# Attention on TensorE: value products issued ahead of later scores, and the turn of the value sums in four single transposes

## The reference, cut to what matters

```python
# x: (2, 1024, 128), 16 heads of 8, two batches: 32 heads
q = x @ Wq
latent_kv = (x @ Wk + x @ Wv) @ W_down_kv
k_rec, v_rec = latent_kv @ W_up_k, latent_kv @ W_up_v
scores = einsum('bhqd,bhkd->bhqk', qh, kh) * scale
decay = exp(-0.01 * 0.01 * abs(idx[:, None] - idx[None, :]))
attn = softmax(clip(scores) * decay)
out = einsum('bhqk,bhkd->bhqd', attn, vh) @ Wo
```

## Time and profile before

| what | value |
|---|---|
| median of 3 runs | 1020.47 us |
| lowest, highest | 1020.0, 1024.17 us |
| profiled execution, its time | 1019.52 us |
| profiled execution, its span | 1017.8 us |
| granted clock of TensorE, mean | 0.989 |
| TensorE busy | 947.4 us (93%) |
| ScalarE busy | 791.9 us (78%) |
| VectorE busy | 765.0 us (75%) |
| GpSimd busy | 235.8 us (23%) |

### The profile page before, as it was taken

How to read it: one execution, slowest core, us unless ns; L and a number is a source line. 1 busy time by engine, 2 the same in 40 slices (tenths; PEclk the granted TensorE clock), 3 DMA queues, 4 the chain that set the end, 5 groups by cost and what they waited for, 6 DMA issues and landing times.

```text
span 1017.8 us, 19514 instructions
## 1 busy us (share of the span) xinstructions
PE 947.4 (93%) x5246; PEld 641.9 (63%) x5246; DVE 765.0 (75%) x1700; ACT 791.9 (78%) x1368; POOL 235.8 (23%) x375
## 2 busy tenths in 40 slices
PE   5498888889889999999999999999998998999997
PEld 2221222222255888888888888888885997888885
DVE  6533333333368899999999999999997887699997
ACT  6599999999968777887787787778785775755554
POOL 3767975554670000000000000000005113100000
PEclk9799999999999999999999999999999999999999
DMA  5659979787722877777767776777631000043421
GB/s 137 183 174 281 284 251 265 233 259 246 250 85 73 305 234 239 251 231 242 253 226 243 252 234 236 253 232 243 244 107 62 1 1 2 19 134 109 129 88 42
DMA packets 96457, 186.50 MB, mean 183 GB/s; under 512 B 10636, under 2 KB 55308, under 8 KB 96396
## 3 DMA queue, kind: packets, MB, share of 16 engines
q1 hardware_dynamic: 96212, 185.33, 56.9%
q10 hardware_dynamic: 192, 0.52, 0.2%
HBM read 149.84 MB, written 35.98 MB: 183 GB/s over the span
## 4 chain that ended last, share of the span: by engine, by line
PE 74%; ACT 15%; DVE 5%; issue 2%; POOL 2%; DMA 1%; ACTq 0%; SPq 0%; DVEq 0%; POOLq 0%
PE bank L1553 30%; PE bank L1566 17%; ACT ring L1033 11%; PE bank L1560 8%; PE bank L1419 8%; PE bank L1441 4%; PE bank L1450 1%; DVE stats L1806 1%; PE bank L1680 1%; PE bank L1690 1%; DMA k_stack<-k_parts 1%; DVE state L2160 1%; POOL rstd L736 1%; DVE bank L1955 1%; POOL m_norm L907 0%
## 5 line engine op out<-in xcount | busy, mean ns | idle before, releaser
L1553 PE MATMUL bank<-xh,w_parts 128*128 128x512 f32 x896 | 276.7, 390 | 1.3 <-ACT xn L1190 1.3
L1123 ACT ACTIVATE bank<-bank 128x512 f32<-128x512 f32 x320 | 186.3, 582 | 90.1 <-PE bank L1553 90.0
L1033 ACT ACTIVATE ring<-bank 128x1024 f32<-128x1024 f32 x256 | 239.5, 1021 | 12.2 <-DVE bank L1955 11.7
L2064 DVE TENSOR_TENSOR bank<-bank,ring 128x512 f32<-128x512 f32 x320 | 223.9, 700 | 26.2 <-ACT bank L1123 3.9
L1566 PE MATMUL bank<-hh,w_parts 128*128 128x512 f32 x768 | 237.1, 390 | 0.0
L2053 DVE TENSOR_TENSOR hl<-bank,hh 128x512 fp32r<-128x512 f32 x320 | 217.9, 681 | 0.1
L1553 PEld LDWEIGHTS bank<-xh,w_parts 128*128 128x128 f32 x896 | 167.2, 188 | 38.5 <-POOL xl L914 1.7
L1117 ACT ACTIVATE hh<-bank 128x512 fp32r<-128x512 f32 x320 | 190.1, 594 | 0.5 <-DVE bank L2064 0.5
L1955 DVE TENSOR_TENSOR bank<-bank,corner 128x128 f32<-128x128 f32 x256 | 63.9, 295 | 167.2 <-PE bank L1419 167.0
L1553 PE MATMUL bank<-xl,w_parts 128*128 128x512 f32 x448 | 174.4, 389 | 0.0
L1566 PEld LDWEIGHTS bank<-hh,w_parts 128*128 128x128 f32 x768 | 144.0, 188 | 30.7 <-ACT hh L1117 1.0
(11 more groups left out here) (320 smaller groups left out, 1023.6 us busy)
## 6 DMA issues: line engine op xcount, KB each, us to landing
ring<-c_rows SPq DMA_DIRECT2D x172, 512.0 KB, 4.8
w_parts<-w_pairs SPq DMA_DIRECT2D x160, 128.0 KB, 2.9
w_pairs<-xh SPq DMA_DIRECT2D x16, 768.0 KB, 5.4
w_pairs<-xl SPq DMA_DIRECT2D x16, 512.0 KB, 3.9
big<-in_w_exp SPq DMA_DIRECT2D x16, 384.0 KB, 5.9
q_stack<-q_parts SPq DMA_DIRECT2D x32, 192.0 KB
w_ffn_parts<-xl SPq DMA_DIRECT2D x16, 384.0 KB, 4.9
w_parts<-w_ffn_parts SPq DMA_DIRECT2D x16, 384.0 KB, 3.1
```

The costliest lines, as they stand in the source:

```text
L1033: act.activation(ring[:, c % RING * S:(c % RING + 1) * S], wide[(m + c) % SB][:], ACT.Exp, bias=-BOUND).then_inc(exp_done, 1)
L1123: act.activation(bank(4 + c % ZB), bank(4 + c % ZB), ACT.Silu).then_inc(silu_ready, 1)
L1553: ins = pe.matmul(out_, w[i], x_[j], start=start and k == 0, stop=stop and k == 2, skip_group_check=not start)
L2064: dve.tensor_tensor(bank(4 + c % ZB), bank(4 + c % ZB), cb[u][:, g * GW:(g + 1) * GW], ALU.mult).then_inc(hid_ready, 1)
```

## The change

In `body`, the products of step p are issued ahead of the scores of step p + 2. `turn` now issues one transpose; it is called at the end of steps 1 to 4, where it follows the scores of that step. The wait for the evacuated sums stands ahead of the first of the four, the signal behind the last, as before. In the last turn after the loop the four are issued one after the other. No other engine's program changes.

```diff
-                def turn(i, s, half_):
+                def turn(i, s, t):
 
-                    if half_ == 0:
+                    if t == 0:
                         ready(pe, evac_ready, i)
-                    for t in range(2 * half_, 2 * half_ + 2):
-                        ins = pe.transpose(bank(7 - s)[:, t * P:(t + 1) * P], evac[1 - s][:, t * P:(t + 1) * P], ident[:])
-                    if half_ == 1:
+                    ins = pe.transpose(bank(7 - s)[:, t * P:(t + 1) * P], evac[1 - s][:, t * P:(t + 1) * P], ident[:])
+                    if t == 3:
                         ins.then_inc(evacT_psum, 1)
 
                 def body(j, b, last=False):
                     for p in range(QT):
+                        products(j, b, p)
                         if not last or p + 2 < QT:
                             two_scores(j, b, p + 2)
-                        products(j, b, p)
-                        if p in (2, 4):
-                            turn(j * 6 + b, b % 2, p // 2 - 1)
+                        if 1 <= p <= 4:
+                            turn(j * 6 + b, b % 2, p - 1)
...
-                for half_ in range(2):
-                    turn(NH // 2, 0, half_)
+                for t in range(4):
+                    turn(NH // 2, 0, t)
```

## The result

The changed kernel takes 1024.2 us (median of 20 runs, 1022.26 to 1028.13), the kernel before 1020.51 us beside it. The ratio is 1.0033, interval 1.0024 to 1.0042: 3.4 us slower, between 2.4 and 4.3 (the two medians themselves are 3.7 us apart). The forecast was 1.0 us slower, 1021.5 in all, with 1019.5 to 1023.5 as its own range. The sign was right and so was the loop that was to cause it, the size was not: 1024.2 lies above that own range, and within the whole one only because that reached to 1025.0, most of the way to rival B.

The account below looks back on a forecast made before the run. ScalarE's exponentials were taken to bound attention. Fifteen passes at 15.00 instead of 14.97 us (0.5) plus 0.5 in the first pass, added to the median 1020.5, gave 1021.5; own range 1019.5 to 1023.5, whole range 1017.6 to 1025.0.

Parts of the forecast that it names:

- rival B: Attention: a wait of 0.07 us exposed in every step, passes of 15.28, 1025.7 us in all; chance 0.08.
- What bounds the stage: Attention: ScalarE's exponentials, 0.92 us apart, set the pace; TensorE's lateness costs 0.25 us of a 14.97 us pass.
- two losses of 0.06: Attention before the change: twice a pass, a pair of transposes delays the next exponential by 0.06 us; the change removes both.
- The loop through the products: Attention: odd exponential, products, scores, even exponential three places on would take 2.80 us against ScalarE's 2.76.
- I take 0.97: Attention, TensorE: time from products' start to scores' start, put at 0.97 us between 0.87 and 0.99.
- taken as 0.04: First products of a pass: two extra waits, for loaded values and finished head, cost 0 to 0.08 us, taken as 0.04.
- its own upper case: Attention: products to scores at 0.99 and both extra waits paid give passes of 15.12, 2.3 us slower.
- The first pass: First attention pass, TensorE at half clock: scores behind products come 0.6 us late; 0.5 us lost.
- The turn behind the scores: Attention steps 1 to 4: a single transpose with handover, some 0.21 us, is covered with 0.14 us of waiting.
- The weight loads pulled ahead: Attention, TensorE: weights loaded ahead of matmuls in flight would make the handover free, products to scores 0.87 us.
- rival A: Attention: the handover is hidden, products to scores takes 0.87, passes 14.74, 1017.6 us in all; chance 0.14.
- Rival C: First attention pass: TensorE's clock rises later, two more half-clock steps, 1023.5 us in all; chance 0.08.

Follow-up runs that it names:

- turn_only: Kernel before with only the turn split into four single transposes at the end of steps 1 to 4, scores still ahead of products; 1017.76 us, ratio 0.9973.
- half_columns: waits_first with each value product taking 256 instead of 512 queries in seven of a pass's eight steps (output not the reference's); 1019.96 us, ratio 0.9986.
- waits_first: Changed kernel with a pass's first products waiting for loaded values and finished head ahead of the exponential, not behind it; 1021.9 us, ratio 1.001.
- written_out: Changed kernel with all sixteen of TensorE's attention passes written out instead of partly run in a hardware loop; 1022.69 us, ratio 1.0011.
- order_only: Kernel before with only the products moved ahead of the scores, the turn still two pairs of transposes after steps 2 and 4; 1023.56 us, ratio 1.003.
- turn_stack: turn_only with the scores of a new pair of heads waiting for their stacks ahead of the exponential; 1018.71 us, ratio 0.9985.

## Why the prediction was right or wrong

*What bounds the stage*: right. ScalarE's 0.92 stood in every run, as the distance wherever nothing was late, and turn_only won the two losses of 0.06 that were read before.

*The loop through the products*: right as a mechanism, shown by half_columns. Its third term, "I take 0.97", was mis-sized: it is 1.00, the upper bound. The loop is 1.02 + 0.05 + 1.00 + 0.76 = 2.83, two steps take 3.75, four pairs and the change of heads 15.08, and the written-out passes take 15.07, 15.08 and 15.01. The prediction has its exponentials come "0.92 and 0.94 apart in turn"; by its own loop, and in the trace, three come 0.92 apart and the fourth has the whole lateness, with the same sum.

*"taken as 0.04"*: the term that failed most. The two waits of the first products cost 0.19 in a looped pass, above the 0.08 that I gave as the most, and nothing in a written-out one. I had read their price off the scores' one extra wait (0.07) and thought it a property of the wait; it depends on which of the waits the weight load itself carries, and that differs between looped and written-out passes. 11 x 0.19 = 2.1 us of the 3 that were missing in the stage; the 0.03 of the handover, less the 0.04 for the waits, makes 15 x (0.12 - 0.04) = 1.2. Together 3.3 against 3.1 (4.1 measured in the stage, 1.0 forecast).

Why the forecast still held as a range: its own upper case, 0.99 and both waits at 0.08, ends at 1023.3, under the 1024.2 measured, and the looped pass of 15.26 is almost rival B's 15.28 by another mechanism. That 1024.2 fell inside the 1025.0 is luck to that extent.

*The first pass*: 0.5 forecast, 0.38 measured, and the nearness is in part chance. The exponential that was to be 0.6 late came 2.05 behind the one before instead of 1.27, 0.78 late (0.14 of it the two waits, since it is 1.91 in waits_first and in written_out); the next even one came 1.39 behind instead of 1.81 and made up 0.42. In waits_first, with the same order of matmuls, the clock rose 5.3 us after the first exponential, not 6.5, and the pass took 16.36, less than before. *The turn behind the scores*: covered, but by 0.01 us and not by the 0.14 that were worked out; a transpose and its handover take 0.30 (101.98 to 102.28), not 0.21, and the pair in order_only, 0.37, stuck out by 0.06, so there was room for 0.31. *The weight loads pulled ahead*, rival A: no handover between products, scores and transposes came out free in any run; the pass of 14.74 was not seen. The rule of the Trainium skill cited there ("TensorE: Matmul & The Clock Gate", Step-by-step: what each phase is for) would, taken alone, have made the handover free; 1.00 against 0.87 says otherwise for these shapes, and the measurement decides. What makes up the 0.13 of the handover no run here separates. Rival B, a wait exposed behind the exponential: its mechanism was there, but once a pass with 0.19 and not in each step with 0.07, hence 2.1 us and not 4.7. Rival C: the clock rose in the first pass as before (mean granted clock of the pass 0.81, before 0.80). That it can fall once behind attention, and that this shifts a profile by 1.5 us, was in no case of mine.

## What to carry to other kernels

When work on a second engine is moved from behind the operation that feeds the first engine to ahead of it, write down the loop from one result to the next operand that it allows: a term of 1 us that was hidden entirely is then on the path, and 0.07 us too much is paid at every turn of it. A gain and a loss in one change are worth taking apart: here the single transposes alone, in the old order, make 1017.76 us against 1020.83 before and have the lowest ratio measured (turn_stack's interval overlaps it). Where a wait can be late, it should be the one that the working instruction itself carries; look at the distance from release to start in the trace before and after, since the order in the source doesn't tell which it is. On TensorE the weight load carried the exponential's wait in the looped passes when that was written last, and in the written-out ones when it was written first; on ScalarE the exponential carried the corner's wait when that was written first.

## What the hardware showed unexpectedly

- Waits behind the deciding one are not free: two with values from the loop's register cost 0.19 us on TensorE. The same two with constants cost nothing in the same source order, since they were joined in one instruction ahead of it, and 0.09 when they were written first (waits_first, written-out passes). On ScalarE a changed order cost 0.06 at each of 128 exponentials, 0.5 us a pass.
- The f32 value products of a step, four in the program and eight in the records, took as long as half of them: 1.00 and 0.98 us until the next kind of matmul. With half of the queries TensorE had finished early enough to be idle for 0.29 us before the scores.
- TensorE's clock fell to 1.2 GHz once behind attention in some profiles and not in others of nearly the same program, worth 1.2 to 2.3 us of 1020 (728.5 to 728.7 against 729.9 to 730.8 behind the last exponential).
